# State scan of a graph network's last layer: the states in PSUM, eight channels at a time

## What is computed

```python
dt  = softplus(dbc[:, :16] @ dt_proj_w.T + dt_proj_b)      # per node, 256 channels
Bm, Cm = dbc[:, 16:32], dbc[:, 32:48]                      # 16 states
dA  = jnp.exp(dt[:, :, None] * A)
dBx = (dt * xc)[:, :, None] * Bm[:, None, :]
def step(h, t):
    dA_t, dBx_t, C_t = t
    h = dA_t * h + dBx_t
    return (h, h @ C_t)
_, y = lax.scan(step, zeros, (dA, dBx, Cm))                # over the nodes, in order
```

## Time and profile before

| what | us |
|---|---|
| median of three runs | 8251.5 |
| lowest and highest run | 8216.29, 8261.37 |
| the profiled execution | 8300.73 |
| span of its instructions | 8299.0 |
| DVE, POOL, PE busy in the span | 4949.6, 4511.4, 3989.6 |
| `attend_and_scan` in the span | from 5883 to 7931 |

### The profile page before, as it was taken

One profiled execution on the slowest core, in us unless ns is written; L12 is line 12 of the kernel. 1 busy time (PEld: TensorE's weight loads), 2 busy tenths in 40 slices (PEclk: granted clock), 3 DMA queues, 4 the chain that ended last, 5 costly groups with the idle time before them and its releaser, 6 DMA issues. The chain is left out here.

```text
span 8299.0 us, 76882 instructions
## 1 busy us (share of the span) xinstructions
PE 3989.6 (48%) x18736; PEld 3170.2 (38%) x18737; DVE 4949.6 (60%) x9260; ACT 1503.5 (18%) x3223; POOL 4511.4 (54%) x4181
## 2 busy tenths in 40 slices
PE   3455344444446666666112122279544445455546
PEld 3233233333335555555001111158433434344434
DVE  7578777777733333333677777656345555566656
ACT  4112111111110001011000000035222222222212
POOL 0500566666646666775566666625436665666521
PEclk7777667766667778777555555579767777777768
DMA  2323455555522222221233233233222322333210
GB/s 80 83 75 120 136 159 150 147 150 156 145 67 76 75 71 68 82 75 53 66 81 87 77 83 83 75 121 123 65 72 84 91 81 74 94 93 89 76 35 12
DMA packets 488326, 753.18 MB, mean 91 GB/s; under 512 B 266063, under 2 KB 341401, under 8 KB 481292
## 3 DMA queue, kind: packets, MB, share of 16 engines
q0 software_dynamic: 221248, 560.96, 24.4%
q10 hardware_dynamic: 72136, 118.30, 4.0%
q1 hardware_dynamic: 194816, 72.51, 3.6%
HBM read 744.81 MB, written 87.48 MB: 100 GB/s over the span
## 5 line engine op out<-in xcount | busy, mean ns | idle before, releaser
L2394 POOL DMA_INDIRECT m_rows<-scratch_gat,m_index x928 | 1181.4, 1273 | 873.3 <-DVE m_work L2677 321.9
L1928 POOL DMA_INDIRECT rel_rows<-scratch_x,rel_index x928 | 1010.0, 1088 | 498.4 <-issue 271.8
L1021 POOL DMA_INDIRECT conv_rows<-scratch_kv,conv_index x928 | 930.4, 1003 | 505.8 <-issue 296.4
L1021 POOL DMA_INDIRECT gat_rows<-scratch_gat,gat_index x928 | 928.9, 1001 | 463.5 <-issue 288.7
L1297 PE MATMUL conv_ps<-conv_work,k_ident 128*128 128x264 f32 x1856 | 675.2, 540 | 842.9 <-DVE conv_work L1097 546.3
L1297 PEld LDWEIGHTS conv_ps<-conv_work,k_ident 128*128 128x128 f32 x1856 | 504.6, 279 | 1013.2 <-issue 877.8
L2193 PE MATMUL rel_ps<-rel_factor,rel_rows 128*128 128x128 f32 x3712 | 611.1, 332 | 179.8 <-issue 98.3
L2193 PEld LDWEIGHTS rel_ps<-rel_factor,rel_rows 128*128 128x128 f32 x3712 | 574.4, 243 | 203.5 <-issue 137.6
L2452 PE MATMUL m_ps<-m_work,k_ident 128*128 128x256 f32 x1664 | 505.5, 473 | 277.2 <-DVE m_work L2677 246.1
L2452 PEld LDWEIGHTS m_ps<-m_work,k_ident 128*128 128x128 f32 x1664 | 398.9, 246 | 377.1 <-issue 302.4
L724 PE MATMUL gat_ps<-k_ident,gat_cur 128*128 128x128 f32 x50 | 17.2, 448 | 1023.0 <-DVE gat_cur L1149 520.1
(11 more groups left out here) (534 smaller groups left out, 8966.3 us busy)
## 6 DMA issues: line engine op xcount, KB each, us to landing
m_bc<-scratch_bc ACTq DMA_DIRECT2D x25, 2048.0 KB
scratch_pairs<-c_logs ACTq DMA_DIRECT2D x25, 1600.0 KB, 6.8
d_pairs<-scratch_pairs SPq DMA_DIRECT2D x25, 1600.0 KB
conv_rows<-scratch_kv,conv_index POOLq DMA_INDIRECT x928
rel_rows<-scratch_x,rel_index POOLq DMA_INDIRECT x928
gat_rows<-scratch_gat,gat_index POOLq DMA_INDIRECT x928
m_rows<-scratch_gat,m_index POOLq DMA_INDIRECT x928
scratch_runs<-e_runs_sb ACTq DMA_DIRECT2D x1, 6453.1 KB
```

The lines of the kernel that those rows point to most:

```text
L1021: pool.indirect_dma_start(out=rows[b][:, s, :], out_offset=None, in_=table, in_offset=bass.IndirectOffsetOnAxis(ap=index[b][:, s:s + 1], a ...
L1928: pool.indirect_dma_start(out=rows[b][:, g, :], out_offset=None, in_=dr["x1"], in_offset=bass.IndirectOffsetOnAxis(ap=index[b][:, g:g + 1] ...
L2394: pool.indirect_dma_start(out=rows[b][:, s, :], out_offset=None, in_=dr["gat3"], in_offset=bass.IndirectOffsetOnAxis(ap=index[b][:, s:s + ...
```

## The change

The state of one k is split in two halves of eight states (the diff's slices `ns`). A tensor `state` of 128x8x128 takes two banks of PSUM. Into it goes the product of `dtx` and B for eight states; the carry is added there, the scan reads and writes it there, the last column is copied out of it, and only its product with C goes to `hs` in SBUF. So each k has two products with B, two adds of the carry, two scans, two copies and two products with C, of half the size; the carry's product and the zeroing of `da` stay single. `outflow` is merged into `scan`. `dtx` moves to PSUM too, into the bank of `prob`.

To free two banks the small tensors share: `ps_t` lies in the bank of `ps_xz`, `ps_o` in that of `ps_y`. So `project` waits for `zz` ahead of its transposes in place of behind them, and `sum_states` waits for `yout` (ACT's copy of `ps_o` of the tile before).

```diff
--- before.py
+++ after.py
@@ -2308,21 +2308,24 @@
         xc, zz = sb("xc", [P, 2, 2 * P]), sb("zz", [P, 2, 2 * P])
         dbc = sb("dbc", [R + 2 * NS, P])
         bc = sb("bc", [P, 2, 2 * NS * P])
-        u, dt, dtx, e, w1, d1, ln, mag = (sb(n, [P, 2 * P]) for n in ("u", "dt", "dtx", "e", "w1", "d1", "ln", "mag"))
+        u, dt, e, w1, d1, ln, mag = (sb(n, [P, 2 * P]) for n in ("u", "dt", "e", "w1", "d1", "ln", "mag"))
         da = spare_room[:, 0:2 * NS * P].rearrange("p (k n c) -> p k n c", k=2, n=NS)
         hs = sb("hs", [P, 2, NS, P])
         last, carry = sb("last", [P, 2, NS]), sb("carry", [P, 2, NS])
         y, yr = sb("y", [P, 2, P]), sb("yr", [P, F])
 
-        bank = [ctx.enter_context(nc.psum_tensor(f"m_ps{k}", [P, 512], F32)) for k in range(8)]
+        bank = [ctx.enter_context(nc.psum_tensor(f"m_ps{k}", [P, 512], F32)) for k in range(6)]
+        NH = NS // 2
+        state = ctx.enter_context(nc.psum_tensor("m_psstate", [P, NH, P], F32))
         ps_t = bank[0][:, 0:F].rearrange("p (k c) -> p k c", k=2)
-        ps_xz = bank[1][:].rearrange("p (k c) -> p k c", k=4)
-        ps_d = bank[2][0:R + 2 * NS, 0:P]
-        ps_dt = bank[2][:, P:3 * P].rearrange("p (k c) -> p k c", k=2)
-        ps_o = bank[3][:, 0:F]
-        ps_y = bank[4][:, 0:F].rearrange("p (k c) -> p k c", k=2)
-        prob = bank[5][:, 0:(S + 1) * H].rearrange("p (s h) -> p s h", h=H)
-        ps_sum = [bank[6][:, 0:F], bank[7][:, 0:F]]
+        ps_xz = bank[0][:].rearrange("p (k c) -> p k c", k=4)
+        ps_d = bank[1][0:R + 2 * NS, 0:P]
+        ps_dt = bank[1][:, P:3 * P].rearrange("p (k c) -> p k c", k=2)
+        ps_y = bank[2][:, 0:F].rearrange("p (k c) -> p k c", k=2)
+        ps_o = bank[2][:, F:2 * F]
+        prob = bank[3][:, 0:(S + 1) * H].rearrange("p (s h) -> p s h", h=H)
+        dtx = bank[3][:, P:P + F]
+        ps_sum = [bank[4][:, 0:F], bank[5][:, 0:F]]
         block = ctx.enter_context(nc.Block())
         LOADS = 9
         per_head, as_heads = "p s (h d) -> p s h d", "p (h d) -> p h d"
@@ -2408,10 +2411,10 @@
 
             def project(t):
                 pe.wait_ge(sems["rows"], t * 16 + 16)
+                if not (isinstance(t, int) and t == 0):
+                    pe.wait_ge(sems["zz"], t)
                 transposed(pe, ps_t, xs, kp["ident"][:]).then_inc(sems["turned"], 1)
                 pe.wait_ge(sems["xt"], t + 1)
-                if not (isinstance(t, int) and t == 0):
-                    pe.wait_ge(sems["zz"], t)
                 for m in range(4):
                     for k in range(2):
                         ins = pe.matmul(ps_xz[:, m, :], w_in[:, k, m * P:(m + 1) * P], xst[:, k, :], start=k == 0,
@@ -2430,6 +2433,7 @@
                 ins.then_inc(sems["dt"], 1)
 
             def sum_states(t):
+                pe.wait_ge(sems["yout"], t + 1)
                 for k in range(2):
                     pe.wait_ge(sems["states"], t * 2 + k + 1)
                     for n in range(NS):
@@ -2581,7 +2585,7 @@
 
         @block.vector
         def _(v):
-            START, PER, CONV = 27, 30, 10
+            START, PER, CONV = 27, 40, 10
             G_PER, G_PRO, G_END = 11, 3, 2
             for b in (FIRST_BUF, SECOND, 0, 1):
                 v.memset(rows[b][:], 0.0).then_inc(released[b], 1)
@@ -2627,21 +2631,22 @@
                 v.wait_ge(sems["spread"], t * 16 + 16)
                 if not (isinstance(t, int) and t == 0):
                     v.wait_ge(sems["sums"], t * 2)
-                b_rows = parity(bc, t)[:, 0:NS * P].rearrange("p (n c) -> p n c", n=NS)
-                st.do(v.tensor_tensor(hs[:, k, :, :], over_slots(dtx[:, k * P:(k + 1) * P], NS), b_rows, ALU.mult))
-                v.wait_ge(sems["decay"], t * 2 + k + 1)
-                st.do(v.tensor_tensor(carry[:, k, :], da[:, k, :, 0], last[:, k, :], ALU.mult))
-                st.add(v.tensor_tensor(hs[:, k, :, 0], hs[:, k, :, 0], carry[:, k, :], ALU.add))
-                st.add(v.memset(da[:, k, :, 0], 0.0))
-                st.wait()
-                hs_k = hs[:, k, :, :].rearrange("p n c -> p (n c)")
-                st.do(v.tensor_tensor_scan(hs_k, da[:, k, :, :].rearrange("p n c -> p (n c)"), hs_k, 0.0, ALU.mult,
-                                           ALU.add))
-                st.do(v.tensor_copy(last[:, k, :], hs[:, k, :, P - 1]))
-
-            def outflow(st, t, k):
-                c_rows = parity(bc, t)[:, NS * P:2 * NS * P].rearrange("p (n c) -> p n c", n=NS)
-                st.do(v.tensor_tensor(hs[:, k, :, :], hs[:, k, :, :], c_rows, ALU.mult))
+                for half in range(2):
+                    ns = slice(half * NH, (half + 1) * NH)
+                    b_rows = parity(bc, t)[:, half * NH * P:(half + 1) * NH * P].rearrange("p (n c) -> p n c", n=NH)
+                    c_rows = parity(bc, t)[:, (NS + half * NH) * P:(NS + (half + 1) * NH) * P].rearrange("p (n c) -> p n c", n=NH)
+                    st.do(v.tensor_tensor(state[:], over_slots(dtx[:, k * P:(k + 1) * P], NH), b_rows, ALU.mult))
+                    if half == 0:
+                        v.wait_ge(sems["decay"], t * 2 + k + 1)
+                        st.do(v.tensor_tensor(carry[:, k, :], da[:, k, :, 0], last[:, k, :], ALU.mult))
+                        st.add(v.memset(da[:, k, :, 0], 0.0))
+                    st.add(v.tensor_tensor(state[:, :, 0], state[:, :, 0], carry[:, k, ns], ALU.add))
+                    st.wait()
+                    flat = state[:].rearrange("p n c -> p (n c)")
+                    st.do(v.tensor_tensor_scan(flat, da[:, k, ns, :].rearrange("p n c -> p (n c)"), flat, 0.0, ALU.mult,
+                                               ALU.add))
+                    st.add(v.tensor_copy(last[:, k, ns], state[:, :, P - 1]))
+                    st.do(v.tensor_tensor(hs[:, k, ns, :], state[:], c_rows, ALU.mult))
                 v.sem_inc(sems["states"], 1)
 
             def finish_y(st, t):
@@ -2710,9 +2715,7 @@
 
                 st = new_steps(v, sems["steps"])
                 scan(st, t, 0)
-                outflow(st, t, 0)
                 scan(st, t, 1)
-                outflow(st, t, 1)
 
                 logits(g, w, 0, SECOND)
                 weigh(g, w, 0, SECOND)
```

## The result

The changed kernel took 8307.6 us at the median (four runs, 8295.3 to 8321.0), the kernel before 8233.9 (four runs, 8205.3 to 8261.4): a ratio of 1.0083, 95% interval 1.0052 to 1.0114. So it is slower by some 0.7%. Forecast were 8263, range 8175 to 8400, counted from 8251.5, the median of the kernel before's first three runs. The single number stood for "no change" (+12 us), but of the three outcomes "slower" had the largest chance, 0.43, and the time came out there. It also lies just above the forecast's own range of 8233 to 8305.

The account below looks back on a forecast made before the run. Middle tiles were taken as bound by POOL's partly held gather stretch plus late reports, the others by DVE's scan. +42 outside the middle and -30 in it gave +12 us on 8251.5: 8263, range 8175 to 8400.

Parts of the forecast that it names:

- Gathers set free: GpSimd's gathers in the scan stage no longer held by DVE; +42 us outside the middle tiles, -30 in them.
- the PSUM and instruction prices: DVE in the scan: PSUM costs nothing, at most 0.007 us per instruction; half product 1.22 us, half scan 2.30.
- (d): DVE instructions on `state` or `dtx`: PSUM dearer, 0.065 us each, 1.3 us a tile, +32 us: 8295; chance 0.07.
- (e): Scan with its second operand in PSUM still holds POOL; middle tiles neither gain nor lose, +42 us: 8293; chance 0.06.
- The split, +2.0 and 3.0 with the product exposed: DVE's scan: halving costs +2.0 us per tile, 3.0 in 22 tiles where the second half product is exposed.
- The ten middle tiles, -30: Tiles with 40 gathers in one stretch: freed gathers gain 3 us per tile, bounds -5 and 0.
- 17.6 us now and 3.0 more then: DVE in middle tiles, from first carry to end of scan stage: 17.6 us before, 20.6 after the change.
- Rival (b): Middle tiles: held gathers let PE's `ps_d` report through; without holds six tiles lose some 20 us, 8401; chance 0.12.
- Rival (c): Middle tiles: another late report (`xz`, `dt`) takes the gain; 0 to +2.4 us per tile, some 8305; chance 0.15.
- rival (a): Middle tiles: PE's reports come amid the second stretch, leaving DVE's path alone; -71 us, 8180; chance 0.20.
- +42: The 15 tiles outside the middle, where the scan is on the path: 2.0 or 3.0 us more each, +42 us.

Follow-up runs that it names:

- e2: Kernel before with the state split in halves of eight channels, all of it in SBUF; ratio 1.0007 to the kernel before.
- e1: Kernel before run once more without any edit, for a second profile; ratio 1.0004.
- e5: Changed kernel run again without any edit, on a second chip; ratio 1.0063 to the kernel before.
- e4: Changed kernel with only `dtx` moved back to SBUF; ratio 1.0011 to the kernel before.
- e7: Changed kernel, chunk 1's gathers waiting for the decays of k = 0, or of k = 1 in tiles with a tail; ratio 0.9877 to the kernel before.
- e10: Changed kernel with four increments of an unread semaphore ahead of each gather; ratio 0.9820 to the kernel before.
- e3: Changed kernel with GpSimd waiting for a tile's decays before gathering its chunk 0; 8419.9 us, ratio 1.0144 to the kernel before.
- e12: Changed kernel with e10's increments and e6's wait together; ratio 0.9758 to the kernel before.
- e6: Changed kernel with chunk 1's gathers waiting for the tile's decays of k = 0; ratio 0.9933 to the kernel before.

## Why the prediction was right or wrong

**Gathers set free, the PSUM and instruction prices: right.** No gather over 1.3 us; product 1.22 forecast, 1.23 measured; scan 2.30 and 2.295 (the 2.07 ns an element came from the difference of two scans, which can't confirm each other by it; e2 and the changed kernel do); DVE's busy time rose by 31 us from the first tile to the last, 32 from e1 to e5, forecast 45. Rivals (d) and (e) are out.

**The split, +2.0 and 3.0 with the product exposed: mechanism right, size a little off.** DVE's chain from the first carry to the end of the last product with C grew from 17.6 to 20.2 us in all tiles but the middle ones. In the changed kernel:

```profile
7286.37 0.18 DVE L2641 TENSOR_TENSOR m_carry<-k_b,m_last 128x16 f32<-128x16 f32 x1 [3.30 <-ACT k_b L2522]
7305.36 1.21 DVE L2649 TENSOR_TENSOR m_hs<-m_psstate,m_bc 128x1024 f32<-128x1024 f32 x1
```

The step had 20.6, as it took 1.0 us per split in full beside the exposed half; the copy, behind which nothing waits, cost less. Of the 2.6 us the later tiles show 1.9 in the first pair of profiles and 2.6 in e5 against e1. The 15 tiles outside the middle and what follows them cost 29.3 us (9.9 + 17.3 + 2.1) and 28.2 (0.4 + 23.4 + 4.4), forecast 42.

**The ten middle tiles, -30: this step failed.** They gave -5 and +13 us. Set against its own working, from the start of the stretch in the tile above: the first carry at 14.1 (forecast 15.7), the end of the scan stage at 41.7 (36.3), the second stretch from 46.8 (41.4) to 67.3 (62.2), the copy of `ps_o` at 69.6 (65.2), the next tile at 88.1 (84). Nearly all of it is one error (the first carry and the report of `ps_o` came 1.6 and 0.7 us sooner than forecast), made in "17.6 us now and 3.0 more then": the chain from carry to product took 27.5 us, not 20.6, since DVE waited 7.48 us for the report of the decays of k = 1. The pauses on both sides of it came out as forecast (5.1 us from the scan's end to the second stretch, 20.6 for 16 gathers, a report 2.3 us behind its end, 18.5 until the next stretch).

The prediction had asked this question for three reports (`ps_d`, `xz`, `dt`), not for that of the decays, which looked safe since in the kernel before it fell behind held gathers. Rival (b) said that the holds let reports through, and priced the loss of `ps_d`'s at +150; that report came as before (5 to 7 us into the tile), so (b) fell in its place, though its idea was the right one. Rival (c), a gain eaten by another late report, is what happened in kind, with `dt` or `xz` named and at most +2.4 a tile.

e4 and e7 remove the 7.5 us, by different breaks (e7 in nine of the ten tiles), and bring the middle tiles to 82 us, below the 84 forecast. With e10's breaks rival (a) came true as well: `flow_out`'s report amid the gathers, and middle tiles of 77 us.

**The sum.** The forecast of +12 was +42 - 30. Measured from the first tile on: +29 - 5 = +24 and +28 + 13 = +41. The second lies within its comparison's interval (34 to 70 us). The first doesn't (43 to 94): 20 us or more of the first comparison are in no kind of tile, and a trace of one execution can't say where they are. That the time fell into the forecast range is in part luck: the range was wide enough for (a) and (b), and of the sum's two terms one came out a third smaller and the other didn't come.

**What stays open.** That a break ahead of the report makes it come in time is shown by five kernels (e3, e4, e7, e10, e12). Why a long unbroken stretch delays it, and makes ACT, PE and, in e10, POOL go on at one instruction in 0.70 or 1.40 us, isn't: it looks as if instructions and reports passed through something that fills up with the gathers and empties in a break of a microsecond. The Trainium skill ("Runtime: NRT & Kernel Launch", Instruction fetch mechanics) says that each engine's instructions are fetched ahead by a DMA queue of its own. The page of the changed kernel has two queues of that kind for the whole span; the table of queues between 6343 and 7831 us, in which the middle and the later tiles lie, has none:

```profile
q8 instruction: 47, 0.77, 0.0%
q14 instruction: 79, 0.65, 0.0%
...
q0 software_dynamic: 32798, 81.37, 20.6%
q10 hardware_dynamic: 8976, 45.01, 7.7%
q1 hardware_dynamic: 24048, 0.69, 0.9%
```

So fetches by these queues are not what holds the engines back there. One rival is untested: every run on record carries a span and a granted clock read from a profile, so none is known to have been taken without recording, and the recording loses more events in the changed kernel (a third of the decays' increments) than in the one before (four of 50). Whether the recording itself has a part in the delay, and with it in the loss and in the gains of e6 to e12, no run can say.

## What to carry to other kernels

Before freeing an engine from stalls, look what runs in them: a stall of one queue can be the only break in which the others report and are supplied, and the gain is then paid back as a wait elsewhere. List every report that is due inside the longer unbroken stretch, those of the neighbours' own work too, not only the ones that were late before. And when a change that ought to help doesn't, add the break by hand: here a wait placed where the data isn't needed yet, or idle increments, turned a loss of 0.7% into a gain of 0.7 to 2.4%. The same wait at another chunk (e3) cost 1.4%, so look which reports fall into the stretch that it makes. Measure such a gain without recording too, which wasn't done here.

## What the runs showed of the hardware

- In an unbroken stretch of gathers (one per 1.30 us) ACT issued an instruction every 0.70 or 1.40 us without a wait, from 16.7 to 19.0 us into the stretch on, and its increment arrived 7.3 to 9.4 us late; with one break of 1.04 us the instructions were 0.30 us apart and the increment came at once. The Trainium skill ("SBUF — State Buffer", Who interferes with whom) says that PE and ACT never wait on anyone; of SBUF's ports that may hold, but ACT was slowed here to one instruction in 1.40 us in place of 0.30.
- Gathers are held one at a time, to the end of the DVE instruction that has two SBUF operands: halving these instructions halved the time held (254 to 117 us) with the same work.
- Four semaphore increments per gather cost POOL nothing between gathers, and a standstill of 1 to 3 us after 8 to 15 of them, ahead of which single increments took 0.70 us in place of 0.02 (e10).
- A scan in PSUM takes as long as one in SBUF (2295 and 2292 ns for 1024 elements, 1228 for 512), and so do products (1232, 1218 and 1225 ns).
